# Rounding P to fp16 and taking its remainder for two steps in one instruction

## What is computed

```python
q = x @ Wq.T ; k_raw = context @ Wk.T ; v_raw = context @ Wv.T
q = _rmsnorm(q) ; k = _rmsnorm(k)                      # per head
scores = jnp.einsum('bhnd,bhmd->bhnm', q, k) * scale
attn = jax.nn.softmax(scores, axis=-1)
out = jnp.einsum('bhnm,bhmd->bhnd', attn, v)
...
x = x + jnp.tanh(g_xattn[0]) * _L0_xattn_ref(_layernorm(x, axis=-1), ctx_2048, Wq, Wk, Wv)
x = x + jnp.tanh(g_ffn[0]) * _L0_ffn_ref(_layernorm(x, axis=-1), w1, w2, w3)
# ffn: weights quantised to -1, 0, 1; sigmoid(x @ w1.T) * (x @ w2.T), then @ w3.T
```

## Time and profile before

| | us |
|---|---|
| median of 3 runs | 2762.47 |
| lowest, highest | 2758.04, 2762.9 |
| the profiled execution, its own time | 2759.16 |
| its span, first to last instruction | 2757.4 |
| TensorE busy | 2648.1 |
| VectorE busy | 1776.7 |
| ScalarE busy | 1520.9 |
| GpSimd busy | 941.8 |

### The profile page before, as it was taken

How to read it: one execution, slowest core, us unless ns; L and a number is a source line. 1 busy time by engine, 2 the same in 40 slices (tenths; PEclk the granted TensorE clock), 3 DMA queues, 4 the chain that set the end, 5 groups by cost and what they waited for, 6 DMA issues and landing times.

```text
span 2757.4 us, 50999 instructions
## 1 busy us (share of the span) xinstructions
PE 2648.1 (96%) x19362; PEld 1943.5 (70%) x19362; DVE 1776.7 (64%) x2808; ACT 1520.9 (55%) x3102; POOL 941.8 (34%) x865
## 2 busy tenths in 40 slices
PE   7998999999999999999999999985899999999999
PEld 5776888888888888888888887774455555554444
DVE  6665787888878888878888888887444444430000
ACT  3444787788877788877788777775211111110000
POOL 4653254443443543544534466765100000000000
PEclk9998999999999999999999999997999999999999
DMA  4345323332332233232323344555633332325442
GB/s 162 106 107 181 97 83 108 97 107 90 120 105 93 86 105 131 79 111 93 106 88 96 106 144 139 166 173 164 199 108 107 105 102 93 104 87 154 145 114 77
DMA packets 229780, 319.70 MB, mean 116 GB/s; under 512 B 101792, under 2 KB 178080, under 8 KB 224800
## 3 DMA queue, kind: packets, MB, share of 16 engines
q1 hardware_dynamic: 229536, 316.44, 36.1%
HBM read 252.17 MB, written 64.23 MB: 115 GB/s over the span
## 4 chain that ended last, share of the span: by engine, by line
issue 35%; POOL 31%; PE 30%; DVE 2%; DMA 1%; ACT 1%; POOLq 0%; DVEq 0%; SPq 0%; ACTq 0%
PE ps L1322 19%; POOL krs L575 13%; PE ps L1349 10%; POOL oinv L596 4%; POOL osum L591 3%; POOL qrs L553 3%; POOL kms L571 2%; POOL osum L594 2%; POOL oatt L601 2%; POOL qms L550 1%; DMA stage<-x_normalised 1%; DVE plo L1073 1%; POOL oinv L598 1%; POOLq L50 0%; PE ps L1226 0%
## 5 line engine op out<-in xcount | busy, mean ns | idle before, releaser
L1226 PE MATMUL ps<-wkhi,chi 128*125 128x512 f32 x1536 | 668.4, 435 | 8.5 <-DVE wklo L882 4.9
L1226 PE MATMUL ps<-wklo,chi 128*125 128x512 f32 x1536 | 607.1, 395 | 0.0
L1226 PE MATMUL ps<-wkhi,clo 128*125 128x512 f32 x1536 | 606.1, 395 | 0.0
L1073 DVE TENSOR_TENSOR plo<-pf,phi 125x448 f16<-125x448 f32 x768 | 535.4, 698 | 79.3 <-ACT phi L794 75.4
L803 ACT ACTIVATE pf<-ps 125x448 f32<-125x448 f32 x768 | 418.1, 544 | 290.9 <-PE ps L1244 273.6
L1322 PE MATMUL ps<-xnTh,w12q 128*128 128x512 f16 (+1 forms) x1408 | 479.5, 354 | 3.8 <-ACT xnTh L819 3.8
L1322 PE MATMUL ps<-xnTl,w12q 128*128 128x512 f16 (+1 forms) x1408 | 478.9, 354 | 0.0
L794 ACT ACTIVATE phi<-pf 125x448 f16<-125x448 f32 x768 | 441.0, 574 | 3.3
L1269 PE MATMUL ps<-val,phi 125*128 125x97 bf16 (+1 forms) x3072 | 357.4, 216 | 25.9 <-DVE plo L1073 25.4
L575 POOL TENSOR_TENSOR krs<-kms,mhalf 125x8 f32<-125x8 f32 x192 | 346.9, 1807 | 15.1 <-POOL kms L571 0.2
L1272 PE MATMUL ps<-val,plo 125*128 125x65 bf16 (+1 forms) x3072 | 345.7, 195 | 0.0
(11 more groups left out here) (95 smaller groups left out, 3633.6 us busy)
## 6 DMA issues: line engine op xcount, KB each, us to landing
craw<-in_ctx SPq DMA_DIRECT2D x193, 500.0 KB, 3.7
gbuf<-in_wffn SPq DMA_DIRECT2D x33, 1024.0 KB, 6.5
wraw<-in_wffn SPq DMA_DIRECT2D x66, 512.0 KB, 6.2
hid<-hidden SPq DMA_DIRECT2D x7, 2816.0 KB, 12.6
hidden<-hh SPq DMA_DIRECT2D x66, 256.0 KB, 2.1
q_stacks<-qTs SPq DMA_DIRECT2D x56, 256.0 KB, 3.5
qT<-q_stacks SPq DMA_DIRECT2D x32, 448.0 KB, 4.8
wkraw<-in_wkv SPq DMA_DIRECT2D x4, 2048.0 KB, 9.4
```

Source lines behind the costliest of these rows:

```text
L1073: dve.tensor_tensor(plo[0:KW, e % 6, :, :], pf[0:KW, e % 6, :].rearrange("p (t n) -> p t n", t=2), phi[0:KW, e % 6, :, :], ALU.subtract).t ...
L1226: mm = pe.matmul(bank(pt)[0:KW, :], a[:, pt, kc, :], w[:, kc, :], start=(kc == 0 and n == 0), stop=(kc == KC - 1 and n == 2))
```

## The change

ScalarE rounds P, and VectorE takes the remainder, once for two S (2 x 448 = 896 elements) instead of once for each. Where one instruction stood in step e + 6, one for the pair (e, e + 1) with e even now stands in step e + 7, which is always an odd step. The exponential stays as it is, one for each S. `phi_ready` and `plo_ready` count pairs, and the waits are rewritten for it: TensorE waits at e and at e + 1 for the same count.

```diff
 (ScalarE)
-                    if attends(k, r, SHIFT + 1):
-                        e = r - SHIFT - 1
+                    if attends(k, r, SHIFT + 2) and (r - SHIFT) % 2 == 0:
+                        e = r - SHIFT - 2
                         R = (u - 1) * NQ + e
-                        act.wait_ge(p_ready, R + 1)
+                        act.wait_ge(p_ready, R + 2)
                         if not (k == 1 and e < 6):
-                            act.wait_ge(pv_done, R - 5)
-                        act.activation(phi[0:KW, e % 6, :, :],
-                                       pf[0:KW, e % 6, :].rearrange("p (t n) -> p t n", t=2), ACT.Copy
+                            act.wait_ge(pv_done, R - 4)
+                        act.activation(phi[0:KW, e % 6:e % 6 + 2, :, :],
+                                       pf[0:KW, e % 6:e % 6 + 2, :].rearrange("p c (t n) -> p c t n", t=2), ACT.Copy
                                        ).then_inc(phi_ready, 1)
...
-                            act.wait_ge(plo_ready, R - 5)
+                            act.wait_ge(plo_ready, (R - 6) // 2 + 1)
 (VectorE)
-                    if attends(k, r, SHIFT + 1):
-                        e = r - SHIFT - 1
-                        dve.wait_ge(phi_ready, (u - 1) * NQ + e + 1)
-                        dve.tensor_tensor(plo[0:KW, e % 6, :, :],
-                                          pf[0:KW, e % 6, :].rearrange("p (t n) -> p t n", t=2),
-                                          phi[0:KW, e % 6, :, :], ALU.subtract).then_inc(plo_ready, 1)
+                    if attends(k, r, SHIFT + 2) and (r - SHIFT) % 2 == 0:
+                        e = r - SHIFT - 2
+                        dve.wait_ge(phi_ready, ((u - 1) * NQ + e) // 2 + 1)
+                        dve.tensor_tensor(plo[0:KW, e % 6:e % 6 + 2, :, :],
+                                          pf[0:KW, e % 6:e % 6 + 2, :].rearrange("p c (t n) -> p c t n", t=2),
+                                          phi[0:KW, e % 6:e % 6 + 2, :, :], ALU.subtract).then_inc(plo_ready, 1)
 (TensorE)
-                        pe.wait_ge(plo_ready, R + 1)
+                        pe.wait_ge(plo_ready, R // 2 + 1)
```

## The result

| | us |
|---|---|
| before, median of 4 runs | 2761.4 |
| changed, median of 4 runs (2793.83 to 2797.62) | 2795.17 |
| ratio | 1.0125, 95% interval 1.0113 to 1.0138 |
| profiled executions, before and changed | 2759.16 and 2793.83 |
| their spans | 2757.4 and 2792.0 |

The account below looks back on a forecast made before the run. TensorE was taken as the bound in 27 of 32 units, so saved ScalarE and VectorE time counts nothing there; late arrivals and clock, 4 + 3 + 0.6 + 1.8 + 10 + 5 + 0 = 24 us on 2762.5, give 2786 us, range 2765 to 2820.

Follow-up runs that it names:

- e3: The changed kernel with VectorE's remainder of a pair moved in front of clo at j = 1; 2804.64 us, ratio 1.0156 to the kernel before.

## What to carry to other kernels

Where the engine that is the bound only waits for results of others, as TensorE does here, two small instructions made into one save nothing, and the first result comes later by what the second part takes and by any step it is held back; add up the margin of every place where it is used, those with rare work in front first. Where two engines exclude one another, a few hundredths of a microsecond decide who goes first, and an edit upstream can move that: either leave more than the length of the other's instruction as margin, or fix the order with a wait. And a delayed instruction delays the queue behind it, so the margin of the next result is to be looked at too (e3).

## What the runs showed of the hardware

- A GpSimd instruction that arrived while VectorE was in clo went next, though VectorE's following instruction stood ready. At t = 4, L591 began 0.02 to 0.06 us ahead of the pair in 24 of the 25 ordinary units, and the pair took 1.63 to 1.67 us in place of 1.09. In the other one it came 0.05 us later, the pair took 1.08, and L591 1.63 in place of 0.74.
- Small instructions on GpSimd are held too. kms on 8 elements for each partition took 0.52 us beside a remainder of VectorE and 0.20 without, krs 1.91 and 1.64.
- A fall of TensorE's clock and a wait for a late operand did not add up. At the starts of groups 1 and 2 the clock fell to a granted 0.66 over 5 us and no wait for plo of over 0.4 us followed; at that of group 3 it stayed at 1.00 and TensorE waited 0.61 and 0.35 us. The three losses were 1.49, 1.30 and 1.44 us.
- The clock did not go by the length of one idle time alone: it fell behind 1.79 us at two places and stayed behind the same 1.79 at a third; it fell behind 2.80 us and stayed behind 2.45 and 2.79.
